# Own engine orders for the last slots of a pipelined vision tower, and another PSUM bank for attention's output while it fills

## The reference

```python
h = tokens(x) + pos                                   # (64, 197, 128)
h = h + attn(layernorm(h))                            # memory = 0.9 * memory + 0.1 * k v^T; out = q @ memory, then Wo
y = layernorm(h)
sel = argmax(softmax(relu(y.mean(1) @ r_w1 + r_b1) @ r_w2 + r_b2))   # 0, 1 or 2, for each image
h = h + gqa(y, *params[sel])                          # 8 heads, softmax over 197 keys, then wo
```

## Time and profile before

| what | value |
|---|---|
| median of 3 runs | 843.01 us (841.98 to 844.24) |
| profiled execution | 847.23 us, its span 845.5 us |
| mean granted clock of TensorE | 0.972 |
| busy of the span: matmuls, VectorE, ScalarE, GpSimd | 93%, 69%, 71%, 47% |
| one slot of the full phase | 11.44 us (first `mix_values` at 640.99 and at 652.43) |
| first `mix_values` of slots 69 to 78 | 744.86, 754.86, 767.80, 778.66, 788.16, 799.05, 807.93, 818.05, 826.36, 835.92 us |
| last `finish` ends | 843.05 us |

### The profile page before, as it was taken

How to read it: one execution, slowest core, us unless ns; L and a number is a source line. 1 busy time by engine, 2 the same in 40 slices (tenths; PEclk the granted TensorE clock), 3 DMA queues, 4 the chain that set the end, 5 groups by cost and what they waited for, 6 DMA issues and landing times.

```text
span 845.5 us, 25686 instructions
## 1 busy us (share of the span) xinstructions
PE 786.9 (93%) x8496; PEld 663.6 (78%) x8496; DVE 580.2 (69%) x1842; ACT 602.9 (71%) x1364; POOL 401.0 (47%) x954
## 2 busy tenths in 40 slices
PE   3777899999999999999999999999999999889886
PEld 2566688888888888888888888888888888767664
DVE  3245677777777777777787777777777877755541
ACT  3456478887788777887877887778878786645553
POOL 1357565555545464555555455655555455411000
PEclk9989899999999999999999999999999999997997
DMA  5545645455555555555555545555555553222200
GB/s 141 142 124 170 181 150 170 139 160 165 162 164 150 150 165 170 160 160 143 160 167 164 165 144 157 161 169 165 150 151 164 167 162 110 89 89 82 90 14 15
DMA packets 138704, 120.53 MB, mean 143 GB/s; under 512 B 12606, under 2 KB 138446, under 8 KB 138574
## 3 DMA queue, kind: packets, MB, share of 16 engines
q1 hardware_dynamic: 136898, 118.34, 47.5%
q10 hardware_dynamic: 1676, 0.57, 0.3%
HBM read 30.99 MB, written 6.46 MB: 44 GB/s over the span
## 4 chain that ended last, share of the span: by engine, by line
PE 83%; DVE 5%; SPq 3%; issue 2%; POOL 2%; ACT 1%; DMA 1%; ACTq 1%; POOLq 1%; DVEq 0%
PE ps L432 12%; PE ps L623 11%; PE ps L572 9%; PE ps L600 7%; PE ps L605 5%; PE ps L545 4%; PE ps L652 4%; PE ps L559 4%; PE ps L503 3%; PE ps L634 3%; PE ps L496 3%; DVE top L841 2%; PE ps L546 2%; PE ps L475 2%; PE ps L515 2%
## 5 line engine op out<-in xcount | busy, mean ns | idle before, releaser
L841 DVE TENSOR_REDUCE top<-ps 99x2 f32<-99x394 f32 x512 | 265.2, 560 | 118.8 <-PE ps L572 118.3
L977 ACT ACTIVATE prob<-ps 99x396 f32<-99x396 f32 x512 | 233.1, 497 | 71.4 <-PE ps L605 71.1
L915 ACT ACTIVATE packed<-img 84x686 f32<-84x686 f32 x128 | 177.9, 1398 | 0.1
L432 PE MATMUL ps<-cols,w_tok 126*128 126x196 f32 x640 | 126.5, 344 | 8.8 <-DMA cols<-packed 7.6
L600 PE MATMUL ps<-top_rows,pick_rows 64*99 64x198 f32 x1024 | 121.1, 267 | 3.0 <-ACT prob L977 3.0
L432 PEld LDWEIGHTS ps<-cols,w_tok 126*128 126x128 f32 x640 | 114.3, 199 | 10.0 <-DMA cols<-packed 8.6
L605 PE MATMUL ps<-stack 64*99 64x198 f32 x1024 | 115.2, 256 | 0.0
L572 PE MATMUL ps<-stack 64*99 64x198 f32 x1024 | 106.9, 288 | 5.2 <-DVE top L841 5.1
L600 PEld LDWEIGHTS ps<-top_rows,pick_rows 64*99 64x99 f32 x1024 | 86.7, 166 | 24.1 <-issue 19.8
L623 PE MATMUL ps<-prob,v_ones 99*32 99x198 f32 (+1 forms) x2048 | 100.9, 337 | 0.1
L366 POOL TENSOR_SCALAR xhat<-h,mv,rstd 99x128 f32<-99x128 f32 x114 | 90.1, 799 | 5.9
(11 more groups left out here) (148 smaller groups left out, 1563.2 us busy)
## 6 DMA issues: line engine op xcount, KB each, us to landing
stack<-qk SPq DMA_DIRECT2D x256, 198.0 KB, 2.4
img<-in_x SPq DMA_DIRECT2D x192, 150.1 KB
cols<-packed SPq DMA_DIRECT2D x128, 160.8 KB
cols<-packed SPq DMA_DIRECT2D x64, 128.6 KB
out<-h SPq DMA_DIRECT2D x64, 49.5 KB
out<-h SPq DMA_DIRECT2D x64, 49.0 KB
w_rows<-in_L_tok_W SPq DMA_DIRECT2D x1, 294.0 KB, 3.4
sets<-in_L_ffn_wo SPq DMA_DIRECT2D x3, 64.0 KB
```

What stands on the lines that cost most here:

```text
L432: last = nc.tensor.matmul(ps[:, CY, 0:N * N], w_tok[0:KROWS, s, :], cols[b.ring % 2][:, :, s, :], start=(s == 0), stop=(s == STEPS - 1))
L841: nc.vector.tensor_reduce(top[:, c // 4, first:first + 2], columns, AX.X, ALU.max, negate=True).then_inc(m_read, 1)
L915: last = nc.scalar.activation(packed[b.ring % 2][:, first:end, :], img[b.ring % IMGS][:, :].rearrange("p (x w) -> p w x", w=P)[:, first:en ...
L977: nc.scalar.activation(prob[:, c, :], ps[0:T, E0 + c % 2, 0:CHUNK], ACT.Exp, scale=DK ** -0.5).then_inc(exp_done, 1)
```

## The change

`DRAINED` is 69. In slots 69 to 78, which are ten, TensorE, VectorE and ScalarE get lists of their own. Three waits are rewritten for the new order: `route_hidden` is now ahead of `turn_top` in its slot, and `turn_top` waits for the routing of its own slot. In the fill, attention's output of images 0 to 6 goes to bank M0, `turn_patches` waits only for ScalarE's `u_ready`, which `attend_out` just ahead has waited for already, and the first `max_scores` waits until VectorE has read the last such output.

```diff
+DRAINED = B + ADDED
@@ turn_patches
-                if added.exists():
+                if added.exists() and b.i + PATCHED < MAXED:
+                    pe.wait_ge(u_ready, added.i + 1)
+                elif added.exists():
                     pe.wait_ge(h1_ready, added.i + 1)
@@ attend_out, and in the same way add_attention on VectorE
+                bank = M0 if b.i + ADDED < MAXED else CZ
-                    last = nc.tensor.matmul(ps[0:T, CZ, t * D:(t + 1) * D], ut[:, t * T:(t + 1) * T], w_vo[:, :],
+                    last = nc.tensor.matmul(ps[0:T, bank, t * D:(t + 1) * D], ut[:, t * T:(t + 1) * T], w_vo[:, :],
@@ route_hidden
-                    pe.wait_ge(top_ready, topped.i + 1)
+                    pe.wait_ge(top_ready, topped.i + (0 if b.i + ROUTED >= DRAINED else 1))
@@ max_scores
                 if b.has(1) or k >= 1:
                     pe.wait_ge(m_read, 8 * b.i + 2 * k)
+                else:
+                    pe.wait_ge(h1_ready, MAXED - ADDED)
@@ turn_top
-                routed, turned = b.back(ROUTED + 1 - TOPPED), b.back(TURNED - TOPPED)
+                routed, turned = b.back(ROUTED - TOPPED), b.back(TURNED - TOPPED)
...
-                elif b.has(1):
+                else:
                     pe.wait_ge(top_ready, b.i)
@@ slot, TensorE
-                for step, b, *which in filling if n.i < MAXED else plan:
+                for step, b, *which in filling if n.i < MAXED else draining if n.i >= DRAINED else plan:
@@ slot, VectorE
+                if n.i >= DRAINED:
+                    plan = [(maximum, maxed, 0), (maximum, maxed, 1), (choose, choosing), (maximum, maxed, 2),
+                            (maximum, maxed, 3), (normalise, ending), (route_relu, routing), (low_halves, projected),
+                            (maximum, maxed, 4), (route_bias, routing), (maximum, maxed, 5), (finish, ending),
...
@@ slot, ScalarE
+                if n.i >= DRAINED:
+                    plan = [(exponent, mixing, 0), (exponent, mixing, 1), (keep_mix, ending), (exponent, mixing, 2),
...
```

More of the change, by code:

```diff
@@ L676, in slot @@
                 ]
-                for step, b, *which in filling if n.i < MAXED else plan:
+                draining = [
+                    (mix_values, ending, 0), (key_scores, mixing, 0), (max_scores, maxed, 0), (mix_values, ending, 1),
+                    (key_scores, mixing, 1), (max_scores, maxed, 1), (row_mix, ending), (project_qk, projected),
+                    (route_hidden, routing), (key_scores, mixing, 2), (max_scores, maxed, 2), (turn_mixed, ending),
+                    (route_logits, routing), (turn_top, topped), (project_v, topped), (project_out, ending),
+                    (key_scores, mixing, 3), (max_scores, maxed, 3),
+                ]
+                for step, b, *which in filling if n.i < MAXED else draining if n.i >= DRAINED else plan:
                     if b.exists():
@@ L773, in add_attention @@
                 dve.wait_ge(kept, b.i + 1)
-                nc.vector.tensor_tensor(h1[b.ring][:, :, :], two(ps[0:T, CZ, 0:2 * D]), h1[b.ring][:, :, :], ALU.add).then_inc(h1_ready, 1)
+                bank = M0 if b.i + ADDED < MAXED else CZ
+                nc.vector.tensor_tensor(h1[b.ring][:, :, :], two(ps[0:T, bank, 0:2 * D]), h1[b.ring][:, :, :], ALU.add).then_inc(h1_ready, 1)
                 dve.wait_ge(add_ready, 1)
@@ L890, in slot @@
                             (normalise2, added), (low_halves, projected)]
+                if n.i >= DRAINED:
+                    plan = [(maximum, maxed, 0), (maximum, maxed, 1), (choose, choosing), (maximum, maxed, 2),
+                            (maximum, maxed, 3), (normalise, ending), (route_relu, routing), (low_halves, projected),
+                            (maximum, maxed, 4), (route_bias, routing), (maximum, maxed, 5), (finish, ending),
+                            (maximum, maxed, 6), (maximum, maxed, 7), (split_top, maxed)]
                 for step, b, *which in plan:
@@ L1022, in slot @@
                             (route_exp, routing), (high_halves, projected), (keep_u, turned), (keep_x2t, added)]
+                if n.i >= DRAINED:
+                    plan = [(exponent, mixing, 0), (exponent, mixing, 1), (keep_mix, ending), (exponent, mixing, 2),
+                            (exponent, mixing, 3), (high_halves, projected), (exponent, mixing, 4), (keep_mixed_t, ending),
+                            (route_exp, routing), (top_row, topped), (exponent, mixing, 5), (exponent, mixing, 6),
+                            (exponent, mixing, 7), (keep_v, topped)]
                 for step, b, *which in plan:
```

## The result

The changed kernel takes 818.93 us (median of 6 runs, 817.55 to 819.84) against 843.62 us of the kernel before on the same chip (6 runs, 841.98 to 847.2): ratio 0.9701, interval 0.968 to 0.9723. That is 24.7 us less, where 17 were forecast (826.0, range 820.5 to 834). The profiled execution took 817.79 us, its span is 816.1. That is 29.4 less than the profiled execution before, more than the medians differ by, because 7.5 us of it lie ahead of the drain (first `mix_values` of slot 69 at 737.37 and at 744.86). So the two drains are compared here, and the medians for the whole.

A forecast was written before the change was run, and what follows sets the result against it. The prediction took the order of TensorE's steps to bound the drain. Gains of 16.2 us there and 0.9 in the fill, 17.1 off 847.23, gave 830.1; less 4.2 for profiling, 825.9, so 826, range 820.5 to 834.

The forecast's parts named there:

- The new wait of slot 70: Slot 70: `project_qk` waits for weights GpSimd copies after `choose`, 1.9 us more, 9.8 us for the slot.
- Two falls of the clock: Drain: two stretches at the lower level, about slot 70's wait and in slots 76 to 78, 2.7 us together.
- The fill: Slots 5 to 11: the new bank removes `turn_patches`' wait for attention's addition, 3.0 us in seven cases; 0.9 us gained.
- the drain's term: From slot 69 to the last vector addition: 82.0 us against 98.19, a gain of 16.2 us.
- The walk: Slots 69 to 78: new order laid out step by step with the old order's durations, 77.8 us at full clock.
- The check of the method on slot 74: Slot 74 in the old order, laid out by the same method: 8.9 us, where the trace has 8.88.
- The allowance of 0.15 a slot: Drain: 1.5 us added for starts that no row gives.
- near chance: Drain, old order: slots 72 and 74 kept clock 1.00 and 71 fell under the same wait, so falling was near chance.
- The clock as bad as before: Drain: 25.5 us stay at the lower level, costing 10 us in place of 2.7; result 833, chance 0.17.
- ScalarE as the bound: Drain: exponent 5 behind `mixed_t` and `top_rows` comes 0.9 later in seven slots, 6.3 us lost; 832, chance 0.13.
- Slower by a clock that stays down: Drain: the clock falls in slot 70's wait and stays at the lower level; result 874, slower at chance 0.02.
- All clocks full and nothing forgotten: Whole kernel: full clock throughout, 20.4 and 0.9 us gained; result 821.7, or 820.5 with the fill's upper end; chance 0.10.

The follow-up runs named there:

- the one move: Kernel before, with `turn_mixed` moved behind the second round of `key_scores` and its ScalarE copy behind exponent 3 in slots 69 to 78: 829.34 us, ratio 0.9828.
- the drain-only one: Changed kernel with the old fill (attention's output in CZ, old wait in `turn_patches`), only the lists of slots 69 to 78 new: 820.54 us, ratio 0.9731.
- an earlier choice: Changed kernel with VectorE's `choose` moved into slot 69, at its end (817.14 us, again 817.08) or ahead of `finish` (816.2 us).
- the kernel with the longer fill: Kernel before, with `turn_patches` in slots 5 to 11 also waiting for VectorE's statistics of the added rows: 849.55 us, ratio 1.0061.
- the fill-only kernel: Kernel before with only the fill changed (bank M0 and the shorter waits), drain in its old order: 844.53 us, ratio 1.0014.
- the fillers: Kernel before with unread matmuls from slot 69 on, three ahead of `turn_mixed`, one ahead of the third `max_scores` where there are maxima: 834.92 us, ratio 0.9894.

## Why the prediction missed: a drain walked too slowly

**What held.** That the order bounded the drain, and that `turn_mixed` behind two more rounds takes away its wait: shown by the one move, where 1.7 us of the 11.5 are left and 14.5 us are won. The new wait of slot 70: 1.82 for 1.9. That slots 71 to 75 keep the full clock: 1.00 in the changed kernel and in the drain-only one. Two falls of the clock, about slot 70's wait and in 76 to 78, at 2.7 us: slots 70 and 78 fell, at 2.2. The fill: L455's wait gone and nearly nothing won (0.9 forecast, between 0.9 won and 3.3 lost by the runs). That `mix_values` starts 0.9 earlier could be neither shown nor denied.

**What failed** is the size of the drain's term: 82.0 us forecast for it, 76.25 in the changed kernel's profile and 74.03 in the drain-only one, so 16.2 us of gain forecast and 21.9 and 24.2 measured. By its three parts:

1. The walk, 77.8 us at the full clock, measured 74.03. In slot 72 it gave 7.94 and the trace 7.44. The order and most waits were right: `key_scores` 1 goes 2.52 after the slot's start (walk 2.45), `row_mix` at 3.25 (3.18). What was wrong are steps taken at the durations of rows, or at spacings read across a wait: `row_mix` 0.68 (is 0.52), `turn_mixed` and `turn_top` 0.32 each (0.22 and 0.17), `project_v` 0.60 (0.44). `project_out` came out at the 0.60 of the walk, but exponent 5 ends 0.06 before the next step there, so it may be ScalarE that sets this distance (in slot 77 the exponent ends 0.28 before, and the distance, behind a wait, is 0.61). That is 0.57 a slot less 0.07 at its start. The check of the method on slot 74 did not catch it, because that slot's length was set by waits for VectorE, behind which a shorter step disappears. In the new order TensorE is busy throughout, and each step counts in full. The slots of the drain-only kernel add up in the same way: 69 took 8.2 for 9.0 (its wait for `log_ready` was 0.3 and not 0.6), 70 9.5 for 9.8, 71 to 73 7.4 for 7.9, 74 and 75 7.2 for 7.7, 76 and 77 within 0.1, 78 6.0 for 6.2; the sum is 3.8.
2. The allowance of 0.15 a slot, 1.5 us, "for starts that no row gives": nothing of the kind showed. It pointed the wrong way.
3. Two falls of the clock at 2.7 us: 2.2 in the changed kernel's profile, none in the drain-only one. The three profiles with an earlier choice have none (drains of 73.04 and 73.07 us at 1.00) or one, in slot 78 (72.75 at 0.98).

For the changed kernel that is 3.8 + 1.5 + 0.5 = 5.8 us, the whole of 82.0 less 76.25. The median lies 7.1 below the forecast; the other 1.3 (2.2, if the fill won nothing) are about the width of its interval, 1.8 us to either side, and have no cause on record.

The kernel before had shorter distances to show. In its full phase TensorE never stands, and `row_mix` takes 0.44 from start to start there (`turn_top` 0.22):

```profile
643.88 0.60 PE L634 MATMUL ps<-ident,mix 128*99 128x128 f32 x4
644.32 0.50 PE L475 MATMUL ps<-x1t,w_kq 128*128 128x198 f32 x2
```

The Trainium skill (TensorE: Matmul & The Clock Gate, "Step-by-step: what each phase is for") has a reason for the first of the three parts: the draining of one matmul overlaps the filling of the next, so a lone one looks longer than its place in a stream. The trace agrees as far as its modelled ends go, 0.68 us of duration beside 0.52 from start to start.

**A reading that was wrong.** The prediction called it near chance whether a slot of the old order falls to the lower level. It is not, for this order. Slots 70, 71 and 73 of the kernel with the longer fill, whose drain is the old one:

```profile
756.93:769.87 12.94, 10.71 (x101) 8.33 (x101) 7.04 (x23) 5.46 (x15) 2.63 (x9) 0.74 0.23 72
769.87:780.69 10.82, 9.24 (x102) 7.35 (x101) 5.96 (x15) 5.53 (x14) 0.93 (x3) 0.84 0.26 86
790.16:801.06 10.90, 9.31 (x102) 7.35 (x101) 6.03 (x15) 5.36 (x14) 0.52 (x2) 0.84 0.27 85
```

The kernel before has 0.74, 0.84 and 0.84 in these slots, and the fill-only kernel 0.73, 0.84 and 0.84. All three profiles have the lower level in slots 70, 71, 73, 75, 77 and 78 and 1.00 in 72, 74 and 76, and each of these slots has the same length in all three within 0.12 us. Slot 69 does differ: 0.85 in the fill-only kernel, 1.00 in the other two. Why from slot 71 on every second slot falls is not shown.

**The rivals.** The clock as bad as before (833) is refuted by 0.96 and 1.00 in the drain. What the prediction priced the lower level at, 10 us for 25.5 us of it or 0.39 each, is about right: the fillers took away 7.7 us in slots 70 to 77, which had been at the lower level for some 21 us, 0.36 each, and 9 by the medians. ScalarE as the bound (832) did not come, but it was nearer than I had put it: in slot 72 exponent 5 starts at 770.19 for 0.50 us, and `key_scores` 3 goes 0.06 after its end. TensorE and ScalarE are level there, in every slot from 71 to 75. Slower by a clock that stays down (874) did not come; slot 70 fell to 0.85 and slot 71 had 1.00. All clocks full and nothing forgotten (821.7, chance 0.10) has the number nearest to the result, but its condition did not hold: the two falls of the forecast are in the changed kernel's profile. The time came near 821.7 because the walk was too slow, not because the clock stayed full.

The gain of 24.7 us thus consists of 8 to 9 for the clock, by the fillers alone, and the rest, some 15, for time in which TensorE stood at the full clock. This split is an estimate, since the two aren't independent: the one move wins 14.5 with both in it.

## What to carry to other kernels

A schedule walked takes start-to-start distances from a stretch in which that engine never waits, not durations and not distances over a wait; and a check of the method has to be made on such a stretch too, since a slot that is paced by another engine hides every error on this one. Where TensorE stands for a microsecond here and there between small groups of matmuls, read the granted clock of each slot, and price the standing twice: the wait, and what the clock loses. Before a step is moved ahead of a long chain on other engines (a choice, a copy of weights), look at whether that chain's head can move too, and into which gap of its engine.

## What the runs showed of the hardware

Three or four useless matmuls in each of ten slots made a kernel 9 us faster (interval 6.8 to 11.0 by the ratio), by holding the clock at 1.00 in slots where it had been 0.74 and 0.84. The falls of the old order came in the same six slots of the drain in three profiles, with the same clocks within 0.01. That is not so for every order: the same slot 70 with the same wait of 1.8 us had clock 0.85 in the changed kernel's profile and 1.00 in the drain-only one's. Four 128-column transposes in a stream cost 0.52 us, and two of 99 columns 0.17 to 0.22, at 2.4 GHz.
